# Three transformer blocks on one core: transposes put behind the scores, and a rearranged start

## The reference

```
x = x + attn_a(layernorm(x))   # Q, K, V = sigmoid(4 * (batchnorm(x @ W) - 1)); t = 1 - mean of a row
                               # A = +-0.9 * exp(-|tQ - tK| / 0.5) + 0.9 by the sign of tQ - tK;  A @ V @ Wo + bo
x = x + ffn(layernorm(x))      # (silu(x @ wg) * (x @ wu)) @ wd, 384 wide, integer weights / 127
x = x + attn_b(layernorm(x))   # causal attention, 16 heads of 64, q, k and v with bias, output Wo and bo
x = x + ffn(layernorm(x))      # the same weights
```

## Time and profile before

| | us |
|---|---|
| median of 3 runs | 383.46 (382.17 to 384.61) |
| the profiled execution, its own time | 382.15 |
| its span in the trace | 380.3 |
| PE busy in the span | 344.0 (90%) |
| DVE busy | 273.7 (72%) |
| ACT busy | 231.4 (61%) |
| POOL busy | 204.6 (54%) |

### The profile page before, as it was taken

The page is one execution under the profiler, slowest core; times in us unless marked ns, Lnnn a source line. Parts: engine busy times, 40 slices in busy tenths (PEclk is TensorE's granted clock), DMA queues, the critical chain, the costliest instruction groups (busy, mean ns, idle before and its releaser), DMA issues.

```text
span 380.3 us, 9882 instructions
## 1 busy us (share of the span) xinstructions
PE 344.0 (90%) x3208; PEld 277.0 (73%) x3208; DVE 273.7 (72%) x1084; ACT 231.4 (61%) x784; POOL 204.6 (54%) x273
## 2 busy tenths in 40 slices
PE   0366699999999999999999999999999999999865
PEld 0265578777877788778878788778887867787654
DVE  1344588897688877886888688887778697767533
ACT  2233357877486758765867658574866476658601
POOL 1616685575468635772578247753574275517420
PEclk9978899999999999999999999999999999999985
DMA  7500000000000000000000000000000000000000
GB/s 275 162 0 0 3 1 3 1 2 3 3 2 0 3 2 2 16 1 2 3 16 2 3 2 3 16 0 2 3 14 4 0 3 16 1 2 3 16 15 14
DMA packets 6418, 5.82 MB, mean 15 GB/s; under 512 B 864, under 2 KB 5856, under 8 KB 6368
## 3 DMA queue, kind: packets, MB, share of 16 engines
q1 hardware_dynamic: 5936, 3.62, 3.3%
q10 hardware_dynamic: 432, 1.57, 1.1%
HBM read 4.15 MB, written 1.05 MB: 14 GB/s over the span
## 4 chain that ended last, share of the span: by engine, by line
PE 80%; DVE 6%; POOL 5%; issue 4%; ACT 2%; DMA 2%; ACTq 0%; POOLq 0%; DVEq 0%
PE bank L380 11%; PE bank L224 10%; PE bank L359 8%; PE bank L294 7%; PE bank L346 7%; PE bank L308 7%; PE bank L344 6%; PE bank L225 6%; PE bank L226 6%; PE bank L284 4%; PE bank L285 3%; PE bank L242 2%; PE bank L273 2%; DMA wqkv<-wqkv_in 2%; POOL wqkv_lo L697 1%
## 5 line engine op out<-in xcount | busy, mean ns | idle before, releaser
L710 POOL TENSOR_TENSOR prob<-prob,row_inv 128x256 f32<-128x256 f32 (+1 forms) x128 | 103.1, 827 | 103.1 <-DVE row_inv L627 103.1
L471 ACT ACTIVATE prob<-neg_s,neg_max 128x256 f32<-128x256 f32 x128 | 63.9, 499 | 0.0
L478 ACT ACTIVATE prob_t<-bank 128x384 f32<-128x384 f32 x64 | 31.5, 492 | 39.5 <-PE bank L359 38.9
L613 DVE CUSTOM_DVE_ANT_0 neg_s<-bank,mask 128x256 f32<-128x256 f32 x128 | 53.4, 417 | 0.0
L637 DVE TENSOR_TENSOR qk<-bank,bqk 128x512 f32<-128x512 f32 x64 | 43.9, 686 | 10.2 <-PE bank L226 10.0
L469 ACT ACTIVATE prob<-neg_s,neg_max 128x128 f32<-128x128 f32 x128 | 50.6, 395 | 0.0
L620 DVE COPY prob_t<-bank 128x384 f32<-128x384 f32 x64 | 35.5, 554 | 18.9 <-PE bank L359 18.5
L380 PE MATMUL bank<-prob_t,v 128*64 128x256 f32 (+1 forms) x512 | 48.9, 332 | 0.0
L380 PEld LDWEIGHTS bank<-prob_t,v 128*64 128x64 f32 x512 | 31.8, 136 | 19.5 <-issue 10.0
L224 PE MATMUL bank<-rt_hi,wqkv_hi 128*128 128x256 f32 x128 | 42.5, 332 | 1.0 <-DVE rt_lo L586 0.9
L359 PEld LDWEIGHTS bank<-ident,prob 64*128 64x128 f32 x768 | 28.9, 138 | 14.9 <-issue 10.3
(11 more groups left out here) (135 smaller groups left out, 781.9 us busy)
## 6 DMA issues: line engine op xcount, KB each, us to landing
wqkv<-wqkv_in ACTq DMA_DIRECT2D x3, 512.0 KB, 5.4
x<-x_in SPq DMA_DIRECT2D x8, 128.0 KB, 5.7
out<-x SPq DMA_DIRECT2D x8, 128.0 KB, 1.8
wo<-wo_in SPq DMA_DIRECT2D x1, 512.0 KB, 4.7
wa<-wa_in SPq DMA_DIRECT2D x1, 192.0 KB, 6.8
wg_i<-wg_in SPq DMA_DIRECT2D x1, 192.0 KB, 5.8
wu_i<-wu_in SPq DMA_DIRECT2D x1, 192.0 KB, 5.8
wd_i<-wd_in SPq DMA_DIRECT2D x1, 192.0 KB, 5.9
```

What stands on the lines that cost most here:

```text
L471: nc.scalar.activation(prob[:, r, e, P:SC], neg_s[:, m % 2, e, P:SC], ACT.Exp, bias=neg_max[:, q, 2 * e + 1:2 * e + 2], scale=-1.0, accum_ ...
L613: nc.vector.tensor_tensor_reduce(out=neg_s[:, m % 2, e, P:SC], in0=S[:, P:SC], in1=mask[:], scale=-SCORE_SCALE, scalar=3e38, op0=ALU.add, ...
L710: nc.gpsimd.tensor_tensor(pr, pr, inv, ALU.mult).then_inc(p_norm, 1)
```

## The change

1. Banks. The ring of three goes. Scores have two banks of their own, `t_banks` hold the transposes, and the sums take turns on bank 1 of `G`. The transposes now wait for both copies of the transposes before them and not for the mask; the scores no longer wait for a copy.
2. Order. Transposes of pair m stand at m + 2.067 on PE, straight behind the scores of m + 2. Behind the scores of an even pair the sums (at an odd number + 3.024) come between the two. The two sums are one step, `weighted_sums`. All other places are new too.
3. Start. ACT issues `wa` and `ga` and nothing else; SP issues `wqkv` behind the integer weights, and x of batches 2 to 7 last. Each third of `wqkv` has its own semaphore. On POOL the first LayerNorm's power comes first, then the batch-norm power; the pieces of `wqkv` come behind.
4. In batch 0 (LayerNorms A, F and B) and in the last LayerNorm P of batch 7, DVE does the two `xn` instructions.

```diff
-    "PE": {"qk": -1.278, "scores": 0.0, "transposes": 2.693, "sum": 3.069},
-    "ACT": {"exp1": 0.39, "exp0": 0.465, "pt0": 2.199, "z": 2.767},
-    "DVE": {"qk": -1.106, "mask": 0.271, "inverse": 1.471, "pt1": 2.768},
-    "POOL": {"norm": 3.377},
+    "PE": {"qk": -1.639, "scores": 0.0, "transposes": 2.067, "sum": 3.024},
+    "ACT": {"exp0": 0.423, "exp1": 0.474, "pt0": 1.835, "sum": 2.809},
+    "DVE": {"qk": -0.571, "mask": 0.989, "inverse": 1.991, "pt1": 3.204},
+    "POOL": {"norm": 5.074},
...
-    "ACT": {"w0": -19.802, "w1": -17.798, "w3": -14.741, "w5": -10.773, "w2": -5.195, "w4": -4.286},
+    "ACT": {"w0": -11.619, "w2": -11.465, "w1": -9.159, "w4": -8.81, "w3": -8.553, "w5": -6.033},
-    "POOL": {"w0": -22.399, "w1": -12.777, "w2": -2.943, "w3": -1.872, "w4": 0.687, "w5": 2.435},
+    "POOL": {"w2": -9.07, "w0": -7.273, "w4": -6.176, "w1": -5.566, "w3": -2.481, "w5": 2.874},
...
-        ring, z_ps, G = bank[0:3], bank[3], bank[4:8]
+        s_banks, t_banks, G = bank[0:2], bank[2:4], bank[4:8]
...
+        def on_vector(k, b):
+            return b == (B - 1 if k == "P" else 0)
...
             sp.dma_start(x[:, 0:T, :], x_view[:, 0:T, :]).then_inc(ld_x[0], 16)
-            for dst, src in ((ga, ga_d), (wa, wa_d)):
-                sp.dma_start(dst[:], src).then_inc(ld_a, 16)
...
+            sp.dma_start(x[:, T:2 * T, :], x_view[:, T:2 * T, :]).then_inc(ld_x[1], 16)
             for dst, src in ((wg_i, wg_d), (wu_i, wu_d), (wd_i, wd_d)):
...
+            for w in range(3):
+                sp.dma_start(wqkv[:, w, :], wqkv_d[:, w, :]).then_inc(ld_w[w], 16)
...
             def scores(m):
-                if m > LAG:
-                    pe.wait_ge(pt_sb_a, m - LAG)
...
             def transposes(m):
                 pe.wait_ge(p_norm, 2 * m + 2)
                 if m:
+                    pe.wait_ge(pt_sb_a, m)
                     pe.wait_ge(pt_sb_b, m)
-                if m + LAG < LAST:
-                    pe.wait_ge(s_masked, 2 * (m + LAG) + 1)
...
-            for w in range(3):
-                act.dma_start(wqkv[:, w, :], wqkv_d[:, w, :]).then_inc(ld_w, 16)
+            act.dma_start(wa[:], wa_d).then_inc(ld_a[0], 16)
+            act.dma_start(ga[:], ga_d).then_inc(ld_a[1], 16)
...
                     if k == "A" and b == 0:
-                        dve.wait_ge(ld_a, 32)
+                        dve.wait_ge(ld_a[1], 16)
+                        nc.vector.tensor_scalar(ga_tmp[:], ga[:, 3, :], EPS, None, ALU.add).then_inc(ga_v, 1)
+                        dve.wait_ge(ld_a[0], 16)
                         link(nc.vector.tensor_copy(wa_hi[:], wa[:]))
                         nc.vector.tensor_tensor(wa_lo[:], wa[:], wa_hi[:].bitcast(F32), ALU.subtract).then_inc(wa_ready, 1)
-                        nc.vector.tensor_scalar(ga_tmp[:], ga[:, 3, :], EPS, None, ALU.add).then_inc(ga_v, 1)
+                    if on_vector(k, b):
...
+                        for j in range(T):
+                            last = nc.vector.tensor_scalar(xn[k][:, j, :], x[:, b * T + j, :], mv[k][:, j, 0:1], rstd[k][:, j, :], ALU.subtract, ALU.mult)
+                        last.then_inc(xn_s[k], 1)
```

More of the change, by code:

```diff
@@ L35 @@
 LAST = B * U
-LAG = 2
 SC = N + P
@@ L53 @@
 }
 JOBS = {
[3 rows of a table removed]
[L58 to L64, removed]
@@ L65 @@
-    "POOL": {"lnsA": -13.523, "sv": -10.311, "stdp": -8.267, "lnsF": -6.527, "lnsB": -2.301, "bo": 8.947, "lnsP": 16.052},
[3 rows of a table added]
+           "dnP": 22.345},
+    "ACT": {"lntA": -12.848, "qkv0": -11.997, "qkv1": -11.906, "qkv2": -11.648, "dist": -11.367, "vwo": -11.129, "lntF": -7.963,
+            "gF2": -7.16, "gF0": -6.784, "gF1": -5.825, "lntB": -3.224, "v1": -0.222, "v0": -0.058, "v2": 3.174, "v3": 5.006,
+            "lntP": 14.457, "gP2": 15.256, "gP0": 15.614, "gP1": 16.438},
+    "DVE": {"lnsA": -15.537, "lntA": -12.201, "mean": -10.714, "sign": -9.84, "aout": -8.746, "lnsF": -7.986, "lntF": -6.295,
+            "gF2": -5.915, "gF0": -4.787, "gF1": -4.473, "dnF": -3.736, "lnsB": -3.227, "lntB": -1.921, "out0": 12.442, "out1": 12.917,
+            "lnsP": 13.222, "lntP": 15.463, "gP2": 16.294, "gP0": 17.777, "gP1": 18.572, "dnP": 23.365},
@@ L66 @@
+    "POOL": {"lnsA": -11.919, "sv": -8.008, "stdp": -6.759, "lnsF": -4.962, "lnsB": -0.781, "bo": 6.994, "lnsP": 17.285},
 }
 ONCE = {
-    "PE": {"bo": -7.196},
-    "ACT": {"w0": -19.802, "w1": -17.798, "w3": -14.741, "w5": -10.773, "w2": -5.195, "w4": -4.286},
-    "DVE": {"bv": -12.471, "bo": -6.68},
-    "POOL": {"w0": -22.399, "w1": -12.777, "w2": -2.943, "w3": -1.872, "w4": 0.687, "w5": 2.435},
-}
-BANK = {"qk": 0, "lntA": 3, "qkv0": 0, "qkv1": 1, "qkv2": 3, "mean": 2, "vwo": 1, "aout": 2, "lntF": 2, "gF0": 2, "gF1": 3, "gF2": 1,
-        "dnF": 2, "lntB": 2, "v0": 0, "v1": 1, "v2": 1, "v3": 3, "bo": 3, "out0": 1, "out1": 3, "lntP": 3, "gP0": 2, "gP1": 3, "gP2": 0,
-        "dnP": 3}
+    "PE": {"bo": -8.766},
@@ new lines @@
+    "ACT": {"w0": -11.619, "w2": -11.465, "w1": -9.159, "w4": -8.81, "w3": -8.553, "w5": -6.033},
+    "DVE": {"bv": -9.647, "bo": -4.491},
+    "POOL": {"w2": -9.07, "w0": -7.273, "w4": -6.176, "w1": -5.566, "w3": -2.481, "w5": 2.874},
+}
+BANK = {"qk": 0, "sum": 1, "lntA": 2, "qkv0": 3, "qkv1": 2, "qkv2": 1, "mean": 2, "vwo": 2, "aout": 3, "lntF": 1, "gF0": 2, "gF1": 3,
+        "gF2": 1, "dnF": 1, "lntB": 3, "v0": 3, "v1": 3, "v2": 1, "v3": 1, "bo": 0, "out0": 3, "out1": 0, "lntP": 2, "gP0": 2, "gP1": 3,
+        "gP2": 1, "dnP": 3}
@@ L85, in order @@
     for name, at in HEADS[engine].items():
-        steps += [((m | 1 if name == "sum" else m) + at, name, m) for m in range(LAST)]
+        steps += [(m + at, name, m) for m in range(LAST) if name != "sum" or m % 2]
     for name, at in JOBS[engine].items():
@@ L667, in side @@
                     nc.gpsimd.tensor_tensor(rstd[k][:, :, 0], var[k][:], minus_half[:], ALU.pow).then_inc(rstd_s[k], 1)
-                    pool.wait_ge(rstd_s[k], b + 1)
-                    if b:
-                        full(pool, f"lnt{k}", b - 1)
-                    for j in range(T):
-                        last = nc.gpsimd.tensor_scalar(xn[k][:, j, :], x[:, b * T + j, :], mv[k][:, j, 0:1], rstd[k][:, j, :], ALU.subtract, ALU.mult)
-                    last.then_inc(xn_s[k], 1)
                     if k == "A" and b == 0:
@@ L676, in side @@
                         nc.gpsimd.tensor_tensor(ga_rs[:], ga_tmp[:], minus_half[:, 0:1].to_broadcast([P, 3]), ALU.pow).then_inc(ga_pow, 1)
+                    if not on_vector(k, b):
+                        pool.wait_ge(rstd_s[k], b + 1)
+                        if b:
+                            full(pool, f"lnt{k}", b - 1)
+                        for j in range(T):
+                            last = nc.gpsimd.tensor_scalar(xn[k][:, j, :], x[:, b * T + j, :], mv[k][:, j, 0:1], rstd[k][:, j, :], ALU.subtract, ALU.mult)
+                        last.then_inc(xn_s[k], 1)
                     if k == "A":
```

78 lines of the change are left out of this document (40 added, 38 removed), and 6 rows, old and new, of the table JOBS.

## The result

The changed kernel takes **362.54 us** (median of 4 runs, 361.32 to 363.35) against 384.03 us beside it: a ratio of 0.944 (95% interval 0.939 to 0.949). Forecast were 360.9 us, range 353.5 to 369; 21.5 us came off where 22.6 were forecast. Measured once more on another occasion, it took 363.68 us, 20.0 less than the kernel before, and the ratio was 0.948 (0.945 to 0.950).

What follows compares the result with a forecast made beforehand. PE's own sequence was taken to bound the middle, a chain over all engines the start. 382.15 - 13.3 + 2.0 - 10.1 (start) - 1.15 (end) = 359.6, with the median 1.3 above: 360.9 us, range 353.5 to 369.

Steps and rivals of the forecast that it cites:

- 0.34 us for a join: Middle, PE: each of 32 transpose sets straight behind scores saves 0.10 + 0.11 + 0.09 + 0.04 us, 10.9 in all.
- 0.20 behind sums: Middle, PE: 13 more transpose sets behind sums each drop one slow full matmul and one way in, 2.5 us together.
- 13.3 in all: Middle: PE time saved by fewer changes between kinds of matmul, 10.9 us behind scores plus 2.5 behind sums.
- rival 2: Middle: joins give little, price belongs to each set or a bare weight load replaces it; 365.4 or 371.8 us; chance 0.22.
- +2.0 for what becomes late: Middle and last pairs: net new PE waits because transposes come some 3 us earlier, 0.8 of it at the last two.
- step e: Start: first transposes now come behind scores 2 and wait for norm 0, behind POOL's LayerNorms; 1.0 us lost.
- Rival 3: Middle: POOL becomes the bound, transposes wait for normalise near LayerNorms; 395 us, chance 0.04; milder form 368 us, 0.06.
- Start (a): First LayerNorm: x lands earlier and DVE makes xn, so the first projections come near 8.3 us; gain 8.4 us.
- Start (b): Moved low pieces on ACT and POOL make aout late by 0.1 us; wqkv's load has 2 us of cover.
- rival 4: Start gains less because the late wqkv holds ACT and so `dist`; 4 us late is 365 us; chance 0.06.
- Start (c), (d): Batch 0: LayerNorm F gains 0.6 us, limited by bo matmuls; LayerNorm B gains 1.9, plus 0.3 from later low pieces.
- End: Last LayerNorm: xn moves to DVE, 1.58 to 0.4 us, all on the chain; gain 1.15 us.

Runs made afterwards that it cites:

- the control: The changed kernel itself, unaltered, measured once more beside the follow-up runs: 363.68 us, ratio 0.948 to the kernel before.

## Why the prediction was right, point by point

- **What bounds.** Right: PE's own sequence in the middle, a chain at the start.
- **0.34 us for a join, 0.20 behind sums, 13.3 in all.** The price is right: in the changed trace 0.10 less at the end of the scores, 0.05 in the transposes; undoing 31 joins cost 0.35 each. The single terms were read in a kernel that has no join. The sum is too high: PE's work between first and last scores shrank by 11.0 us.
- **The bare weight load (rival 2).** Not there. L343 to the transposes is 0.43 us, exactly two passes of 256 columns, and the transposes are shorter, not 0.14 longer. Their first load starts at 154.60 us, while L343 is in flight until 154.98 (`154.60 0.61 PEld L355 LDWEIGHTS bank<-ident,prob 64*128 64x128 f32 x12`). The Trainium skill's rule ("TensorE: Matmul & The Clock Gate", Part 3: Packing small matmuls), that a load overlaps only matmuls of other row groups, is not borne out in this place.
- **+2.0 for what becomes late.** Between first and last scores 3.05 of the 13.3 are missing, against 2.2 forecast there (2.0 less 0.8 for the last transposes, and 1.0 of step e). That looks like 0.85 us of error and is two larger ones with opposite signs: idle time grew by only 0.8, for 2.2, and the work fell 2.3 short. That the middle comes out so near is partly luck. A steady batch (scores 24 to 32) went from 41.06 to 39.72 us, 1.34, where 4 x 0.34 and 13/8 x 0.20 give 1.69. 0.18 of the lack is the sums' wait for the shared bank, of which I had written that the copy is over in time: true of the copy, but gP2, which holds the same bank, was not looked at. The rest, 0.17 a batch, is work and not settled; one part is that aout now stands ahead of scores, where its eight matmuls take 0.99 us instead of 0.81 ahead of full ones, 0.09 more than the way in. PE's wait for `prob` in the middle was 0.5 us. The slots were forecast well (5.5, 3.1, 4.9, 7.2, 5.9, 3.3, 6.2, 3.8 us from scores 24 on), but the two tightest places had 0.85 and 0.89 us to spare (transposes 24 and 25) and not 1.2 and 1.5.
- **Rival 3.** Its mechanism is real and near: 1.45 us less lead cost 8.5 us of waits, 0.62 us more work a pair 4.6 us in time. The change itself stays clear of it, by 0.85 us.
- **Start (a).** 8.05 for 8.4. x landed at 4.24 instead of 3.9, and DVE's two xn take 0.60 instead of 0.4, a mis-sized term since I took L550 as its measure.
- **Start (b).** This step failed: 0.1 forecast, 1.8 measured. I had placed POOL's low parts beside DVE's `less` and casts and costed them as independent; `signed` came 1.24 us late by that, and `stdp` beside the copy of bv cost 0.37. The cover of wqkv's load was not 2 us: the second third landed at 11.46 us, not near 9, and ScalarE used it at 12.07. In the control it landed at 12.28 and ScalarE waited 0.44 us, so rival 4 was near.
- **Start (c), (d).** From aout of batch 0 to the transposes of F 1.05 us were gained for 0.6, as the bo matmuls took 3.34 us instead of 3.62; from there to those of B 1.5 of the 1.9. Then 0.3 was lost to the first scores instead of 0.3 gained, `stdp` holding aout of batch 1 for 1.2 us.
- **Start (e).** The first transposes waited 0.47 us, not 1.0.
- **End.** xn itself 0.98 of 1.15. The other 1.1 is luck: the last twelve matmuls ran at full rate, 1.58 us instead of 2.90 in the trace before, and the transposes ahead of them took 0.44 instead of 0.69; against that, 0.5 was lost between the last scores and the last variance (0.8 forecast, but for transposes that wait), where the sums wait 1.2 us for the shared bank.

The errors are of both signs: 2.6 too much at the start, 0.85 too much in the middle, 1.75 too little at the end, so that 21.5 and 22.6 lie nearer than the steps do. By the control, whose first scores come 1.5 us later, the start was 4.2 too much.

## What to carry to other kernels

Where TensorE is full, read the steps from start to start at each border between full, 64-row and 64-column matmuls; a border costs about 0.1 us on either side of it, and putting row-tiled groups next to each other gives that back, if their banks let them start. Before a step is called free because another engine is idle, look at what VectorE runs in the same stretch. And a wait that the profile shows as 1 us may be one that the present order hides: its price is that of the order which you want.

## What the runs showed that was not expected

- GpSimd's two-input instructions stopped two of VectorE's with one input in SBUF: `less` 1.12 against 0.62 us, a cast 1.42 against 0.35, back to 0.62 and 0.35 when the GpSimd work was moved. The Trainium skill says why ("SBUF — State Buffer", its terms: a port pair that the two share, held by one for a whole instruction); the trace agrees.
- TensorE's steps in the first 20 us are those of the low level of 1.2 GHz (0.21 us for 256 columns against 0.12), though the profile's granted clock reads 1.00 there. In that stretch the column and the steps disagree, and the steps decide.
- 17 matmuls that nobody reads went with a faster kernel, a ratio of 0.934 against 0.940 without them. The intervals touch, so the traces carry this: from the first transposes of LayerNorm F (20.64 against 22.02 us) on, each step of the start comes earlier.
